# The recurrent steps of a two-block network: bf16 pairs for the diagonals of the tanh recurrence, and gates summed in PSUM in the GRU and the LSTM

## The chip, the cores and the metric

One Trainium2 chip, one of its cores. The metric is the device time of one execution of the whole program, in microseconds (us). It is one program with seven stages in a row, each closed by a barrier of all engines.

## What is computed

The input is `x` (16 sequences of 128 steps of 128 features) and a condition vector per sequence, `cond`, which is the first hidden state of three recurrences. The program computes

```python
x = x + mamba(rnn(x, cond))          # tanh recurrence, then a state-space scan
x = x + ffn(gru(x, cond))
x = x + gla(proj(cond, x))           # gated linear attention
x = x + moe(lstm(x, cond))
```

Three of the stages are recurrences over 128 time steps, where a step needs the hidden state of the step before:

```python
# tanh recurrence
h = tanh(h @ Wh + x_t @ Wx + b)
# GRU
reset, update = split(sigmoid(concat([x_t, h]) @ W + b))
m = x_t @ Wx + bx + reset * (h @ Wh + bh)
h = update * h + (1 - update) * tanh(m)
# LSTM
i, f, o = sigmoid(...); g = tanh(...)       # four gates of x_t @ Wx + b + h @ Wh
c = f * c + i * g
h = o * tanh(c)
```

## The kernel before, in words

Features lie on the 128 partitions and the 16 sequences (`N`) along the free axis, so one hidden state is a 128x16 tile. The order of work is written out by hand for each engine, and semaphores carry every dependence: `e.wait_ge(vec, ...)` holds the engine's queue until VectorE has counted that far. Register work (addresses that depend on the loop's counter, values to wait for) stands in the same queues as `ISA` or `REGISTER_ALU`. A recurrence is a loop whose body holds several steps: 8 in the tanh recurrence, 16 (`STEPS`) in the other two.

**The tanh recurrence** (`rnn`) reproduces the reference's sums in a set order of additions, which makes a step long: about 40 us. To get the exact products of a weight row with h, h is cut into three bf16 pieces (`pieces`, lines 122 to 140), and for each piece a "diagonal" of 128x512 is built (L127): the identity, folded to 32 columns (`id32`, float32), times the piece, broadcast along the columns. VectorE's order in `pieces` is: cast of h to piece 0 (L131), remainder (L134), diagonal 0 (L127), cast 1 (L138), remainder, diagonal 1, cast 2, diagonal 2. TensorE (`h_product`, L263) multiplies them with the weights: 12 matmuls with diagonal 0, 8 with diagonal 1, 4 with diagonal 2, each group after a wait on `diagh`. ScalarE copies the four banks out (L395). VectorE, behind `pieces`, does the prefix sums of a later step's input part (`x_prefix(g)`: a scan at L497 and an add at L501), and then waits for ScalarE's fourth copy before the prefix scan of h's products (`prefix_odd(R)`, also L497). The rest of the step (differences, chains, the tanh written out in some 40 small VectorE operations) follows on VectorE.

**The GRU** (`gru`) first computes the input part of all gates for all steps into `gx` (three blocks of 128x2048). Then, for each step: TensorE multiplies h with the weights of reset and update and with `gwh` (three float32 matmuls of 16 columns, L998; the trace shows each as two), and counts `prod` once, after the third; it then issues 6 (`WARM`) matmuls of 512 columns on an idle tile whose result nobody reads (L1001). VectorE adds the input part to both gates (L1028); ScalarE takes one sigmoid of both (L1013); VectorE computes reset times the third product (L1031), adds the input part (L1034); ScalarE takes the tanh (L1015); VectorE computes h - th (L1036), times update (L1038), plus th (L1040), which is the new h and releases TensorE.

**The LSTM** (`lstm`) has the same form: four matmuls (L1080), one count, 6 idle matmuls (L1083), one addition of the input part for four gates (L1110), a sigmoid of three gates (L1095) and a tanh of one (L1096), f*c (L1113), i*g (L1115), their sum (L1117), a tanh (L1098), and o times it (L1119), the new h.

## Time and profile before

| what | value |
|---|---|
| time, median of 3 runs | 8900.65 us (8898.45 to 8903.1) |
| the profiled execution | 8898.33 us, its span 8896.5 us |
| tanh recurrence, loop | 249 to 5407 us |
| GRU, loop | 7548.0 to 7951.3 us |
| LSTM, loop | 8255.0 to 8631.0 us |
| busy over the span: PE, DVE, ACT | 70%, 85%, 48% |

The engines are PE (TensorE), DVE (VectorE), ACT (ScalarE), POOL (GpSimd) and SP. In a row of the timeline the first number is the start in us from the start of the span, the second the duration in us, then engine, line of the kernel, operation, `out<-in`, shapes and count; in brackets how long the engine had been idle, and what released it. A row with `x4` is four instructions merged: its duration is from the first one's start to the last one's end. Each loop has 128 steps.

### The profile page before, as it was taken

What the parts mean: (1) busy time and instruction counts of PE and PEld (TensorE: products, weight loads), DVE (VectorE), ACT (ScalarE), POOL (GpSimd) and SP (SyncE); (2) the same over time, 40 slices, a digit from 0 to 9 for tenths busy, and PEclk for the clock granted to TensorE, in tenths of its full rate; (3) what the DMA queues carried; (4) which work ended last, traced back from release to release, by engine and by line L of the source; (5) the groups of instructions that cost most, each with busy time, mean ns of one, the idle gap of its engine ahead of it and who ended that gap; (6) DMA issues with size and microseconds to landing.
All of it is one profiled execution on the core that took longest, in us unless ns stands there. A gap on an engine that the chain in (4) does not pass through costs nothing. (4 is left out here: it accounts for less than half of the span.)

```text
span 8896.5 us, 108600 instructions
## 1 busy us (share of the span) xinstructions
PE 6269.1 (70%) x33921; PEld 2486.1 (28%) x34193; DVE 7600.0 (85%) x12570; ACT 4291.4 (48%) x4428; POOL 1329.7 (15%) x1111
## 2 busy tenths in 40 slices
PE   5677777676767676767676764488888887662779
PEld 1222222222222222222222221122222222331443
DVE  5999999999999999999999996899999997336223
ACT  3666666665656665656665663233333332112222
POOL 0000000000000000000000000377777774000000
PEclk8888888888888888888888887799999999995999
DMA  0000000000000000000000000000000000000000
GB/s 6 1 1 1 1 1 1 1 1 1 1 1 1 1 1 1 1 1 1 1 1 1 1 1 22 17 3 4 4 4 4 4 4 3 0 6 3 3 14 5
DMA packets 14002, 27.97 MB, mean 3 GB/s; under 512 B 3665, under 2 KB 11602, under 8 KB 12434
## 3 DMA queue, kind: packets, MB, share of 16 engines
q1 hardware_dynamic: 13586, 22.47, 0.9%
q8 instruction: 256, 4.19, 0.2%
q14 instruction: 160, 1.31, 0.0%
HBM read 15.12 MB, written 7.34 MB: 3 GB/s over the span
## 5 line engine op out<-in xcount | busy, mean ns | idle before, releaser
L901 POOL TENSOR_TENSOR hc<-hh,cg 128x512 f32<-128x512 f32 x1024 | 1296.2, 1268 | 506.9 <-DVE hh L884 506.9
L829 ACT ACTIVATE ps_m<-ps_m,aneg 128x508 f32<-128x508 f32 x1024 | 673.4, 658 | 1188.6 <-DVE hh L884 1063.5
L884 DVE TENSOR_TENSOR_SCAN hh<-ps_m,bx 128x512 f32<-128x512 f32 x1024 | 1232.9, 1209 | 0.0
L800 PE MATMUL ps_m<-hc,pick 128*128 128x512 f32 x2048 | 1051.1, 597 | 2.1 <-POOL hc L901 0.8
L508 DVE TENSOR_TENSOR_SCAN co<-rx_d 128x772 f32<-128x772 f32 x544 | 915.4, 1745 | 0.0
L508 DVE TENSOR_TENSOR_SCAN co<-rh_d 128x3088 f32<-128x3088 f32 x128 | 843.8, 6592 | 31.8 <-ACT rh_d L366 28.6
L263 PE MATMUL r_ps<-rh_diag,whq 32*128 32x512 bf16 x3072 | 360.1, 624 | 666.9 <-DVE rh_diag L127 611.5
L866 DVE TENSOR_TENSOR bx<-ps_m,bg 128x512 f32<-128x512 f32 x1024 | 675.3, 664 | 45.9 <-PE ps_m L813 45.8
L439 POOL TENSOR_TENSOR r_gate<-ident 128x1 f32<-128x1 f32 x16 | 5.7, 356 | 4576.1 <-PE r_ps L255 4576.1
L255 PE MATMUL r_ps<-wdiag,xsp 32*128 32x512 bf16 x3312 | 311.4, 528 | 517.8 <-DVE rh_gain L171 186.4
L274 PE MATMUL r_ps<-rh_diag,whn 32*128 32x512 bf16 x4608 | 438.5, 548 | 267.9 <-ACT rh_pd L395 267.9
L281 PE MATMUL r_ps<-rh_s,negid 128*128 128x512 f32 x1024 | 524.3, 658 | 85.2 <-DVE rh_s L501 85.1
L811 PE MATMUL ps_m<-rows,ones 128*128 128x512 bf16 x944 | 371.0, 393 | 249.1 <-ACT ps_m L829 248.4
L281 PE MATMUL r_ps<-rx_s,negid 128*128 128x512 f32 x1096 | 507.9, 607 | 7.9 <-DVE rx_s L501 7.9
L366 ACT ACTIVATE rx_d<-r_ps 128x1024 f32<-128x1024 f32 x274 | 402.3, 1550 | 212.3 <-PE r_ps L287 212.3
L284 PE MATMUL r_ps<-rx_pd,ident 128*128 128x512 f32 x1096 | 492.7, 592 | 0.0
L395 ACT ACTIVATE rh_pd<-r_ps 128x512 f32<-128x512 f32 x512 | 266.1, 604 | 456.9 <-PE r_ps L263 456.6
L360 ACT ACTIVATE rx_d<-rx_s 128x2048 f32<-128x2048 f32 x137 | 417.7, 3049 | 106.6 <-DVE xwt L526 102.9
L284 PE MATMUL r_ps<-rh_gain,ident 128*128 128x512 f32 x1024 | 460.2, 592 | 0.0
L398 ACT ACTIVATE rh_sg<-r_ps 128x2048 bf16<-128x2048 f32 x128 | 240.3, 1878 | 452.4 <-PE r_ps L274 452.4
L800 PEld LDWEIGHTS ps_m<-hc,pick 128*128 128x128 f32 x2048 | 389.8, 191 | 173.4 <-POOL hc L901 21.6
L497 DVE TENSOR_TENSOR_SCAN rx_s<-rx_pd 128x1040 f32<-128x1040 f32 x137 | 317.7, 2319 | 137.7 <-ACT rx_pd L354 102.2
(389 smaller groups left out, 11206.2 us busy)
## 6 DMA issues: line engine op xcount, KB each, us to landing
rows_scratch<-pc SPq DMA_DIRECT2D x48, 128.0 KB
rows<-rows_scratch SPq DMA_DIRECT2D x128, 48.0 KB
ew<-in_e SPq DMA_DIRECT2D x3, 1024.0 KB, 6.8
co<-in_x_dn SPq DMA_DIRECT2D x1, 1024.0 KB, 4.8
xcur<-in_x_dn SPq DMA_DIRECT2D x1, 1024.0 KB
out_x<-xcur SPq DMA_DIRECT2D x1, 1024.0 KB, 3.9
qi<-in_f_q SPq DMA_DIRECT2D x1, 384.0 KB, 3.1
xpw<-in_xp_t SPq DMA_DIRECT2D x1, 257.0 KB
```

The costliest lines, as they stand in the source:

```text
L274: ins = e.matmul(ps[:, bank0 + b, :], whn[rows(b), q, :], h_mov(b, r), start=False, stop=(i == 8), skip_group_check=True)
L281: e.matmul(ps[:, bank0 + b, :], negid[:], piece(F, "s", b), start=True, stop=False)
L284: e.matmul(ps[:, bank0 + b, :], ident[:], diff(b), start=False, stop=False)
L360: e.activation(F["at"][:, :, :, 2::3], pairs(F["s"][:, :, 2:K2]), ACT.Copy).then_inc(done, 1)
L366: e.activation(remainder_slots(F, first, count, odd), remainder_sums(bank0, first, count, odd), ACT.Copy).then_inc(done, 1)
L508: return e.tensor_tensor_scan(co[:, at], F["d"][:, 0, 1:][:, at], F["d"][:, 1, 0:N * LX][:, at], 0.0, ALU.add, ALU.add)
L800: e.matmul(ps[:, 6, :], pick[:, 128 - un:256 - un], hc[un % NHC][:], start=False, stop=True, skip_group_check=True).then_inc(summed, 1)
L811: e.matmul(ps[:, un % 2, :], ones3[:], rows[0][b][:, j, :], start=True, stop=True).then_inc(dt_bc, 1)
L829: e.activation(da[un % NDA][:, :, 1:T], ps[:, un % 2, :].rearrange("p (n t) -> p n t", n=NG4)[:, :, 1:T], ACT.Exp, scale=aneg[:, 0:1]).the ...
L866: e.tensor_tensor(bx[un % NBUF][:], ps[:, 2 + un % 2, :], bg[:], ALU.mult).then_inc(driven, 1)
L884: e.tensor_tensor_scan(hh[un % NBUF][:], da[un % NDA].rearrange("p n t -> p (n t)"), bx[un % NBUF][:], 0.0, ALU.mult, ALU.add).then_inc(sc ...
L901: e.tensor_tensor(hc[un % NHC][:], hh[un % NBUF][:], cg[:], ALU.mult).then_inc(weighted, 1)
```

## The change

Three parts.

1. In `rnn`, the identity is kept in bf16 and repeated for all 16 sequences (`idn`, 128x16x32, one copy in the setup), and each piece of h is written twice side by side (`part` is 128x3x16x2). A diagonal is then a product of two bf16 operands, read in pairs of neighbours. A cast writes 32 elements where it wrote 16. The order of the instructions stays.
2. In `gru` and `lstm`, VectorE copies the next step's input part into PSUM (`seed`), and the matmuls of the gates add onto it (`start=False`). The banks alternate between even and odd steps. ScalarE reads its sums directly from PSUM. The product with `gwh` in the GRU keeps its own bank.
3. The gates are counted and read one by one. In the GRU TensorE's order is reset, `gwh` product, update, with a count after each; the new state is `update*h + sigmoid(-a)*th`, so that `update*h` (`old`) and `1 - update` (`new`, a second ScalarE sigmoid with scale -1) don't wait for the tanh. In the LSTM the input and forget gates are counted first, then the other two. `WARM` is 5 instead of 6.

The diff, cut to its core (the casts and diagonals, the loops of `gru`, the loops of `lstm`):

```diff
-        id32 = sb("id32", [128, KB])
+        id32 = sb("id32", [128, KB]); idn = sb("idn", [128, N, KB], BF16)
-        R.update(part=sb("rh_part", [128, 3, N], BF16), rest=sb("rh_rest", [128, 2, N]),
+        R.update(part=sb("rh_part", [128, 3, N, 2], BF16), rest=sb("rh_rest", [128, 2, N]),
...
+            halves = lambda x: x.rearrange("p n (a c) -> p n a c", c=2)
             def diagonal(q):
-                return tl.inc(e.tensor_tensor(F["diag"][:, q], id32[:].unsqueeze(1).to_broadcast([128, N, KB]),
-                                              F["part"][:, q, :].unsqueeze(2).to_broadcast([128, N, KB]), ALU.mult))
+                return tl.inc(e.tensor_tensor(halves(F["diag"][:, q]), halves(idn[:]),
+                                              F["part"][:, q].unsqueeze(2).to_broadcast([128, N, KB // 2, 2]), ALU.mult))
+            def cast(q, x):
+                return tl.inc(e.tensor_tensor(F["part"][:, q], x.unsqueeze(2).to_broadcast([128, N, 2]),
+                                              nought[:].unsqueeze(2).to_broadcast([128, N, 2]), ALU.add))
...
-WARM = 6
+WARM = 5
...
 # gru, TensorE
-                        e.wait_ge(vec, t * KV + 1)
+                        at = 3 * (step % 2)
+                        e.wait_ge(vec, t * KV + V0)
-                        for q in range(3):
-                            i = e.matmul(ps[:, q, 0:N], gw[:, 1, q * D:(q + 1) * D] if q < 2 else gwh[:], h, start=True, stop=True)
-                        i.then_inc(prod, 1)
+                        e.matmul(ps[:, at, 0:N], gw[:, 1, 0:D], h, start=False, stop=True, skip_group_check=True).then_inc(prod, 1)
+                        e.matmul(ps[:, at + 2, 0:N], gwh[:], h, start=True, stop=True).then_inc(prod, 1)
+                        e.matmul(ps[:, at + 1, 0:N], gw[:, 1, D:2 * D], h, start=False, stop=True, skip_group_check=True).then_inc(prod, 1)
 # gru, ScalarE
-                        e.wait_ge(vec, t * KV + 2)
-                        e.activation(sg[:], gate[:], ACT.Sigmoid).then_inc(act, 1)
-                        e.wait_ge(vec, t * KV + 4)
+                        e.wait_ge(prod, t * KP + 1)
+                        e.activation(reset[:], ps[:, at, 0:N], ACT.Sigmoid).then_inc(act, 1)
+                        e.wait_ge(prod, t * KP + 3)
+                        e.activation(upd[:], ps[:, at + 1, 0:N], ACT.Sigmoid).then_inc(act, 1)
+                        e.activation(new[:], ps[:, at + 1, 0:N], ACT.Sigmoid, scale=-1.0).then_inc(act, 1)
+                        e.wait_ge(vec, t * KV + V0 + 2)
                         e.activation(th[:], r2[:], ACT.Tanh).then_inc(act, 1)
 # gru, VectorE
+                def seed(t, at):
+                    e.tensor_copy(ps[:, at:at + 2, 0:N], gxt[:, 0:2, bass.ds(t, 1), :].rearrange("p q a n -> p q (a n)")).then_inc(vec, 1)
...
-                        e.wait_ge(prod, t + 1)
-                        e.tensor_tensor(gate[:], ps[:, 0:2, 0:N], gxt[:, bass.ds(t, 1), 0:2, :].rearrange("p a q n -> p (a q) n"),
-                                        ALU.add).then_inc(vec, 1)
+                        e.wait_ge(prod, t * KP + 2)
                         e.wait_ge(act, t * KA + 1)
...
+                        seed(t + 1, 3 - at)
                         e.wait_ge(act, t * KA + 2)
-                        e.tensor_tensor(r3[:], at(gh, t), th[:], ALU.subtract).then_inc(vec, 1)
-                        e.wait_ge(vec, t * KV + 5)
-                        e.tensor_tensor(r4[:], r3[:], sg[:, 1, :], ALU.mult).then_inc(vec, 1)
-                        e.wait_ge(vec, t * KV + 6)
-                        e.tensor_tensor(gh[:, bass.ds(t + 1, 1)].rearrange("p a n -> p (a n)"), r4[:], th[:], ALU.add).then_inc(vec, 1)
+                        e.tensor_tensor(old[:], at_t(gh, t), upd[:], ALU.mult).then_inc(vec, 1)
+                        e.wait_ge(act, t * KA + 4)
+                        e.tensor_tensor(r4[:], new[:], th[:], ALU.mult).then_inc(vec, 1)
+                        e.wait_ge(vec, t * KV + V0 + 5)
+                        e.tensor_tensor(at_t(gh, t + 1), r4[:], old[:], ALU.add).then_inc(vec, 1)
...
 # lstm, TensorE
-                        for q in range(4):
-                            i = e.matmul(ps[:, q, 0:N], lwh[:, q * D:(q + 1) * D], h, start=True, stop=True)
-                        i.then_inc(prod, 1)
+                        for q, bank, lo in ((0, 0, 0), (1, 0, N), (3, 1, N), (2, 1, 0)):
+                            i = e.matmul(ps[:, at + bank, lo:lo + N], lwh[:, q * D:(q + 1) * D], h, start=False, stop=True,
+                                         skip_group_check=True)
+                            if q in (1, 2):
+                                i.then_inc(prod, 1)
 # lstm, ScalarE
-                        e.wait_ge(vec, t * KV + 2)
-                        e.activation(s3[:], gate[:, 0:3, :], ACT.Sigmoid).then_inc(act, 1)
-                        e.activation(gg[:], gate[:, 3, :], ACT.Tanh).then_inc(act, 1)
+                        e.wait_ge(prod, t * KP + 1)
+                        e.activation(keeps[:].rearrange("p a n -> p (a n)"), ps[:, at, 0:2 * N], ACT.Sigmoid).then_inc(act, 1)
+                        e.wait_ge(prod, t * KP + 2)
+                        e.activation(gg[:], ps[:, at + 1, N:2 * N], ACT.Tanh).then_inc(act, 1)
+                        e.activation(out_[:], ps[:, at + 1, 0:N], ACT.Sigmoid).then_inc(act, 1)
...
```

How it moves the instructions. First VectorE in one step of the GRU loop, before (`gate` is the sum of gates and input part, the first `r` r1, the second r2, then r3 and r4):

```order
L1028 REGISTER_ALU [waits g_prod]
L1028 TENSOR_TENSOR gate<-ps_g,gx 128x32
L1030 ISA
L1031 SCALAR_TENSOR_TENSOR r<-ps_g,gb,sg 128x16 [waits g_act]
L1033 ISA
L1034 ISA [waits g_vec]
L1034 TENSOR_TENSOR r<-r,gx 128x16
L1035 REGISTER_ALU
L1036 TENSOR_TENSOR r<-gh,th 128x16 [waits g_act]
L1037 REGISTER_ALU
L1038 TENSOR_TENSOR r<-r,sg 128x16 [waits g_vec]
L1039 REGISTER_ALU
```

and with the change (`COPY ps_g` is the seed of the next step):

```order
L1049 ISA [waits g_prod]
L1050 SCALAR_TENSOR_TENSOR r<-ps_g,gb,reset 128x16 [waits g_act]
L1052 ISA
L1053 ISA [waits g_vec]
L1053 TENSOR_TENSOR r<-r,gx 128x16
L1041 ISA
L1041 COPY ps_g<-gx 128x2x16
L1055 REGISTER_ALU
L1056 TENSOR_TENSOR old<-gh,upd 128x16 [waits g_act]
L1057 REGISTER_ALU
L1058 TENSOR_TENSOR r<-new,th 128x16 [waits g_act]
L1059 REGISTER_ALU
```

The addition of `gate` at the head is gone, and the copy into PSUM stands behind r2 with register work ahead of it; behind it come `old` and the product with the tanh, each after its own wait for ScalarE.

ScalarE in the first step of a turn of the GRU loop, before and, in the second fence, with the change (a table load stands at the head of every turn, 16 steps):

```order
L1013 ACT_TABLE_LOAD
L1013 ACTIVATE sg<-gate 128x32 [waits g_vec]
L1014 REGISTER_ALU
L1015 ACTIVATE th<-r 128x16 [waits g_vec]
L1012 ISA
```

```order
L1024 ACT_TABLE_LOAD
L1024 ACTIVATE reset<-ps_g 128x16 [waits g_prod]
L1025 REGISTER_ALU
L1026 ACTIVATE upd<-ps_g 128x16 [waits g_prod]
L1027 ACTIVATE new<-ps_g 128x16
L1028 ISA
L1029 ACTIVATE th<-r 128x16 [waits g_vec]
```

The one sigmoid of both gates, released by VectorE, has become three of one gate each, released by TensorE; the tanh stands behind all three.

VectorE in one step of the LSTM loop, before and, in the second fence, with the change:

```order
L1110 REGISTER_ALU [waits l_prod]
L1110 TENSOR_TENSOR lgate<-ps_l,lgx 128x64
L1112 ISA
L1113 TENSOR_TENSOR lfc<-ls,lcc 128x16 [waits l_act]
L1114 REGISTER_ALU
L1115 TENSOR_TENSOR lig<-ls,lgg 128x16 [waits l_act]
L1116 ISA
L1117 TENSOR_TENSOR lcc<-lfc,lig 128x16 [waits l_vec]
L1118 REGISTER_ALU
L1119 ISA [waits l_act]
L1119 TENSOR_TENSOR gh<-ltc,ls 128x16
```

```order
L1144 TENSOR_TENSOR lfc<-lkeeps,lcc 128x16 [waits l_act]
L1136 ISA
L1136 COPY ps_l<-lgx 128x2x32
L1146 REGISTER_ALU
L1147 TENSOR_TENSOR lig<-lkeeps,lgg 128x16 [waits l_act]
L1148 ISA
L1149 TENSOR_TENSOR lcc<-lfc,lig 128x16 [waits l_vec]
L1150 REGISTER_ALU
L1151 REGISTER_ALU [waits l_act]
L1151 TENSOR_TENSOR gh<-ltc,lout 128x16
```

The addition at the head is gone, and the copy into PSUM stands between f*c (`lfc`) and i*g (`lig`), again with register work ahead of it.

## Rows read from the trace of the kernel before

**Rows 1.** Windows: us, busy (x count) of PE, PEld, DVE, ACT, POOL, clock, DMA.
```profile
249.00:5407.00 5158.00, 3668.78 (x24975) 1414.72 (x25092) 4977.77 (x8576) 3163.82 (x2448) 25.64 (x64) 0.83 0.00 1
7548.00:7951.30 403.30, 272.15 (x1504) 150.58 (x1536) 144.34 (x769) 67.17 (x264) 0.00 (x0) 1.00 0.00 0
8255.00:8631.00 376.00, 300.55 (x1760) 179.13 (x1792) 109.58 (x641) 82.34 (x392) 0.00 (x0) 1.00 0.00 0
```

**Rows 2.** Groups by line, VectorE: name, shapes, count, busy us, mean ns.
```profile
L127 DVE TENSOR_TENSOR rh_diag<-id,rh_part 128x512 bf16<-128x512 f32 x387 | 265.8, 687 | 4.4
...
L171 DVE TENSOR_TENSOR rh_gain<-rh_gain,xq 128x352 f32<-128x352 f32 x128 | 66.3, 518 | 0.0
...
L178 DVE TENSOR_TENSOR rh_gain<-cf,rh_gain 128x176 f32<-128x176 f32 x128 | 42.7, 334 | 0.0
...
L871 DVE COPY bg<-bm 128x512 f32 x4 | 1.8, 460 | 0.8 <-issue 0.3 <-DVE hh L884 0.2
```

**Rows 3.** Timeline, one tanh step: start us, us, engine, line, operation.
```profile
2704.64 0.17 DVE L131 TENSOR_TENSOR rh_part<-h,nought 128x16 bf16<-128x16 f32 x1
...
2704.95 0.68 DVE L127 TENSOR_TENSOR rh_diag<-id,rh_part 128x512 bf16<-128x512 f32 x1
...
2705.69 2.75 PE L263 MATMUL r_ps<-rh_diag,whq 32*128 32x512 bf16 x24 [5.50 <-DVE rh_diag L127]
...
2707.26 2.32 DVE L497 TENSOR_TENSOR_SCAN rx_s<-rx_pd 128x1040 f32<-128x1040 f32 x1
...
2708.46 2.07 ACT L395 ACTIVATE rh_pd<-r_ps 128x512 f32<-128x512 f32 x4 [3.50 <-PE r_ps L263]
...
2710.75 2.32 DVE L497 TENSOR_TENSOR_SCAN rh_s<-rh_pd 128x1040 f32<-128x1040 f32 x1
```

**Rows 4.** Timeline, the first tanh step.
```profile
248.39 2.75 PE L263 MATMUL r_ps<-rh_diag,whq 32*128 32x512 bf16 x24 [0.56 <-ACT xwT L388]
...
253.26 2.33 DVE L497 TENSOR_TENSOR_SCAN rh_s<-rh_pd 128x1040 f32<-128x1040 f32 x1 [2.34 <-ACT rh_pd L395]
```

**Rows 5.** Timeline, one GRU step.
```profile
7702.84 0.61 PE L998 MATMUL ps_g<-gh,gw 128*128 x4 [1.11 <-DVE gh L1040]
...
7703.31 0.37 PE L998 MATMUL ps_g<-gh,gwh 128*128 x2
...
7703.53 1.46 PE L1001 MATMUL ps_g<-g_idle 128*128 128x512 bf16 x6
...
7704.03 0.23 ACT L1013 ACTIVATE sg<-gate 128x32 f32<-128x32 f32 x1 [2.16 <-DVE gate L1028]
7704.30 0.23 DVE L1031 SCALAR_TENSOR_TENSOR r<-ps_g,gb,sg 128x16 f32<-128x16 f32 x1 [0.30 <-ACT sg L1013]
...
7704.89 0.22 ACT L1015 ACTIVATE th<-r 128x16 f32<-128x16 f32 x1 [0.63 <-DVE r L1034]
...
7705.35 0.17 DVE L1038 TENSOR_TENSOR r<-r,sg 128x16 f32<-128x16 f32 x1
...
7705.99 0.61 PE L998 MATMUL ps_g<-gh,gw 128*128 x4 [1.00 <-DVE gh L1040]
```

**Rows 6.** Timeline, one LSTM step.
```profile
8402.33 1.06 PE L1080 MATMUL ps_l<-gh,lwh 128*128 x8 [0.56 <-DVE gh L1119]
...
8403.78 0.24 ACT L1095 ACTIVATE ls<-lgate 128x48 f32<-128x48 f32 x1 [1.91 <-DVE lgate L1110]
8403.92 0.20 ACT L1096 ACTIVATE lgg<-lgate 128x16 f32<-128x16 f32 x1
...
8404.16 0.18 DVE L1115 TENSOR_TENSOR lig<-ls,lgg 128x16 f32<-128x16 f32 x1
...
8405.25 1.06 PE L1080 MATMUL ps_l<-gh,lwh 128*128 x8 [0.56 <-DVE gh L1119]
```

**Rows 7.** Timeline, ScalarE where a GRU loop turn ends.
```profile
7698.97 1.28 ACT L1013 ACT_TABLE_LOAD   x1 [0.26 <-issue]
```

**Rows 8.** One tile's instructions, the GRU's PSUM: ns min/median/max, starts.
```profile
L989 PE MATMUL ps_g<-xcur,gw x16: 592/592/1220, 7534.5 to 7543.2; 128*128 128x512 f32 x16
```

More of the change, by code:

```diff
@@ L124, in pieces @@
         def pieces(tl, e, F, src, dep=None):
+            halves = lambda x: x.rearrange("p n (a c) -> p n a c", c=2)
             def diagonal(q):
-                return tl.inc(e.tensor_tensor(F["diag"][:, q], id32[:].unsqueeze(1).to_broadcast([128, N, KB]),
-                                              F["part"][:, q, :].unsqueeze(2).to_broadcast([128, N, KB]), ALU.mult))
+                return tl.inc(e.tensor_tensor(halves(F["diag"][:, q]), halves(idn[:]),
[3 more added lines that the diff above has]
+                                              nought[:].unsqueeze(2).to_broadcast([128, N, 2]), ALU.add))
             if dep is not None:
                 tl.wait(dep)
-            i = tl.inc(e.tensor_tensor(F["part"][:, 0, :], src, nought[:], ALU.add))
+            i = cast(0, src)
             for q in (1, 2):
                 tl.wait(i)
-                j = tl.inc(e.tensor_tensor(F["rest"][:, q - 1, :], src if q == 1 else F["rest"][:, 0, :], F["part"][:, q - 1, :],
+                j = tl.inc(e.tensor_tensor(F["rest"][:, q - 1, :], src if q == 1 else F["rest"][:, 0, :], F["part"][:, q - 1, :, 0],
                                            ALU.subtract))
@@ L137, in pieces @@
                 tl.wait(j)
-                i = tl.inc(e.tensor_tensor(F["part"][:, q, :], F["rest"][:, q - 1, :], nought[:], ALU.add))
+                i = cast(q, F["rest"][:, q - 1, :])
             tl.wait(i)
@@ L462, in _ @@
                 i = tl.inc(e.tensor_tensor(id32[:], id32[:], ident[:, KB * b:KB * (b + 1)], ALU.add))
+            tl.wait(i)
+            tl.inc(e.tensor_copy(idn[:], id32[:].unsqueeze(1).to_broadcast([128, N, KB])))
             tl.inc(e.memset(xpc[:, :, T * N:], 0.0))
@@ L966, in gru @@
         gw = sb("gw", [128, 2, 2 * D]); gwx = sb("gwx", [128, D]); gwh = sb("gwh", [128, D]); gb = sb("gb", [128, 4])
-        gx = sb("gx", [128, 3, COLS])
-        gate = sb("gate", [128, 2, N]); sg = sb("sg", [128, 2, N]); r1 = sb("r1", [128, N]); r2 = sb("r2", [128, N])
-        th = sb("th", [128, N]); r3 = sb("r3", [128, N]); r4 = sb("r4", [128, N])
+        gx = sb("gx", [128, 3, COLS + N])
+        reset = sb("reset", [128, N]); upd = sb("upd", [128, N]); new = sb("new", [128, N])
+        r1 = sb("r1", [128, N]); r2 = sb("r2", [128, N]); th = sb("th", [128, N]); old = sb("old", [128, N]); r4 = sb("r4", [128, N])
         idle = sb("g_idle", [128, 512], BF16)
@@ L1049, in lstm @@
         lx = sb("lx", [128, 4 * D]); lwh = sb("lwh", [128, 4 * D]); lb = sb("lb", [128, 4])
-        gx = sb("lgx", [128, 4, COLS])
-        gate = sb("lgate", [128, 4, N]); s3 = sb("ls3", [128, 3, N]); gg = sb("lgg", [128, N]); cc = sb("lcc", [128, N])
+        gx = sb("lgx", [128, 4, COLS + N])
+        keeps = sb("lkeeps", [128, 2, N]); out_ = sb("lout", [128, N]); gg = sb("lgg", [128, N]); cc = sb("lcc", [128, N])
         ig = sb("lig", [128, N]); fc = sb("lfc", [128, N]); tc_ = sb("ltc", [128, N])
@@ L1102, in _, with seed @@
                 e.memset(idle[:], 0.0).then_inc(warm, 1)
+                e.memset(gx[:, :, COLS:], 0.0).then_inc(warm, 1)
                 e.wait_ge(moved, 16)
                 e.memset(cc[:], 0.0).then_inc(vec, 1)
-                gxt = gx[:].rearrange("p q (t n) -> p t q n", n=N)
+                gxt = gx[:].rearrange("p (b q) (t n) -> p t b q n", n=N, q=2)
+                def seed(t, at):
+                    e.tensor_copy(ps[:, at:at + 2, 0:2 * N].rearrange("p b (q n) -> p b q n", n=N),
+                                  gxt[:, bass.ds(t, 1)].rearrange("p a b q n -> p (a b) q n")).then_inc(vec, 1)
+                seed(0, 0)
                 with e.Fori(0, T // STEPS) as block:
@@ L1108, in _ @@
                         t = STEPS * block + step
-                        e.wait_ge(prod, t + 1)
-                        e.tensor_tensor(gate[:], ps[:, 0:4, 0:N], gxt[:, bass.ds(t, 1)].rearrange("p a q n -> p (a q) n"),
-                                        ALU.add).then_inc(vec, 1)
                         e.wait_ge(act, t * KA + 1)
-                        e.tensor_tensor(fc[:], s3[:, 1, :], cc[:], ALU.mult).then_inc(vec, 1)
+                        e.tensor_tensor(fc[:], keeps[:, 1, :], cc[:], ALU.mult).then_inc(vec, 1)
+                        seed(t + 1, 2 - 2 * (step % 2))
                         e.wait_ge(act, t * KA + 2)
-                        e.tensor_tensor(ig[:], s3[:, 0, :], gg[:], ALU.mult).then_inc(vec, 1)
-                        e.wait_ge(vec, t * KV + 4)
+                        e.tensor_tensor(ig[:], keeps[:, 0, :], gg[:], ALU.mult).then_inc(vec, 1)
+                        e.wait_ge(vec, t * KV + V0 + 3)
                         e.tensor_tensor(cc[:], fc[:], ig[:], ALU.add).then_inc(vec, 1)
-                        e.wait_ge(act, t * KA + 3)
-                        e.tensor_tensor(lh[:, bass.ds(t + 1, 1)].rearrange("p a n -> p (a n)"), tc_[:], s3[:, 2, :], ALU.mult).then_inc(vec, 1)
+                        e.wait_ge(act, t * KA + 4)
+                        e.tensor_tensor(lh[:, bass.ds(t + 1, 1)].rearrange("p a n -> p (a n)"), tc_[:], out_[:], ALU.mult).then_inc(vec, 1)
 AXX = mybir.AxisListType.X
```

32 lines of the change are left out of this document (20 added, 12 removed).

## The prediction

> **What bounds the kernel now.** I read the windows of the three recurrent loops first [rows 1], then the groups by line [rows 2] and the timelines of single steps [rows 3 to 6]. The tanh loop takes 5158 us and VectorE is busy for 4978 of them: 40.3 us a step, VectorE's to give. The GRU takes 403.3 us (3.15 a step) with VectorE busy 144, ScalarE 67, and TensorE 272, of which most is idle work; the LSTM takes 376.0 us (2.94 a step), busy 110, 82 and 301. No engine is full there: a step is a chain of short operations, each waiting for the one before. So in the first loop I ask what VectorE saves and what it then waits for; in the other two I add up the chain.
>
> **The diagonals.** A 128x512 diagonal takes 0.69 us [rows 2], 387 in all, three a step. The trace has no product of two 16-bit operands. The nearest rows: a copy of 512 elements at 0.46 us, which shows VectorE taking two elements at a time; and, for an operation that takes as many steps as 256 elements, 0.42 us, interpolated between 176 (0.334) and 352 (0.518) [rows 2]. The upper end is no change, 0.69. I take 0.46. The wider casts add 16 elements each, at (0.518 - 0.334)/176 us that is 0.02.
>
> VectorE alone would save 3 x 0.23 - 0.05 = 0.64 us a step. The path does not. In rows 3 the cast starts at 2704.64, diagonal 0 at +0.31; TensorE starts at 2705.69, 0.06 after its end, and takes 2.75; ScalarE follows after 0.02, and VectorE's scan of h's products starts at 2710.75, +6.11. TensorE's 2.75 are not a wait for diagonals 1 and 2: in the first step all three were long there, and it took 2.75 too, with the scan 4.87 after TensorE's start and held by ScalarE [rows 4]. So only diagonal 0 shortens that path. With the change the scan can start at 0.31 + 0.02 + 0.46 + 0.06 + 4.87 = +5.72. VectorE arrives there at +2.62 (the input's scan, 2707.26) - 0.64 + 3.49 (from that scan to h's, 2710.75) = +5.47, and now waits 0.25 for ScalarE's fourth copy. The gain is 6.11 - 5.72 = 0.39 us a step, **50 us** in 128. Behind the scan nothing changes length; the next waits for TensorE and ScalarE count from it. Ends: at 0.42 a diagonal it is 0.43, 55 us; at 0.69 VectorE's path gives +6.16, 6 us lost.
>
> The Trainium skill, "VectorE: DVE Perf Modes", section "The perf-mode tier table", gives a tensor_tensor of 16-bit operands two elements a cycle; by its formula (256 + 151)/0.96 GHz a diagonal would be an estimated 0.42 us and the term 55 us. No row here shows it.
>
> **The GRU.** In rows 5 TensorE's first pass starts at 7702.84; four passes take 0.61 and each 0.26, so they start 0.12 apart, the fifth at +0.47 (7703.31), and the sixth ends at +0.84. The reset product (two passes) is thus ready at +0.38, the second product at +0.61, the third at +0.84. ScalarE's wait behind TensorE was 0.02 in rows 3; VectorE's here 0.13 (from +0.84 to the sigmoid at +1.19 there are 0.35, of which the addition and its hand-over take 0.22). I give ScalarE 0.05: reset runs +0.43 to +0.65. VectorE needs it and the second product (+0.61 + 0.13), and has register work between the two waits: r1 at +0.76, against +1.46 before (7704.30). From there to the tanh 0.59 as before: +1.35, end +1.57. ScalarE's two other sigmoids start at +0.89 and 0.14 later (two in a row start so far apart in rows 6) and end at +1.25, before r2. h - th falls away: r4 started 0.24 after the tanh's end (7705.11 to 7705.35) and can start after 0.04, +1.61; from r4 to the next matmul 0.64 as before: +2.25 against 3.15.
>
> The seed is the term no row shows: nothing of VectorE writes PSUM here. It stands between r2 (from about +1.14) and `old`, whose cover is the tanh's round trip, up to +1.61. At the cost of an operation of 32 elements, about 0.19 (0.334 less 144 elements), with 0.12 of register work ahead, seed and `old` fill that cover to the brim; I let r4 slip by 0.05. Gain 0.90 - 0.05 = 0.85 a step, **109 us**. Ends: no slip, 115 us; a seed as dear as the 512-element copy (0.46), 0.3 of slip, 77 us.
>
> **The LSTM.** In rows 6 the passes start at 8402.33, the last ends at +1.06; the second gate is ready at +0.61 as above. The first sigmoid is over at +0.66 + 0.24 = +0.90, f*c goes to +1.12, the seed behind it. The tanh of g starts at +1.06 + 0.05, takes 0.20, and i*g follows at +1.35 against +1.83 (8404.16). From there to the next step 1.09 as before; the third sigmoid has 0.4 of room before the last tanh. The seed, twice as large, ends about when i*g could start: 0.03 of slip. Gain 0.45, **58 us**. Ends: 61 us, and 36 us with a seed of 0.46.
>
> **What is added.** The table load at each turn of a loop starts 0.26 after the last tanh and takes 1.28 [rows 7]: it ends 1.54 behind that tanh. The next reset sigmoid will be wanted 0.04 + 0.64 + 0.43 = 1.11 behind it: 0.4 late; in the LSTM about 0.3. Seven turns each: 5 us lost, hidden before by the longer step. The setup copy, two memsets and the first seeds: 1 us. `WARM` 5 saves nothing: the idle matmuls, 0.22 apart (1.46 less 0.38 over 5), end 0.69 + 5 x 0.22 + 0.16 = 1.95 into a step of 2.3, so they delay nobody; 6 would have ended at 2.17.
>
> **Sum.** 50 + 109 + 58 - 6 = 211. The profiled execution took 8898.3 us (span 8896.5, 1.8 around it), so 8687; the median of the runs is 2 us above it: **8689 us**.
>
> **Rivals.**
> 1. *The seed is dear.* Speaking for it: no row of VectorE writing PSUM, and both covers are used up in my own sum. Against: adding the gates from PSUM fitted into 0.22. With 0.46 a seed: GRU 77, LSTM 36, so 54 less: 8743.
> 2. *The diagonals stay at 0.69.* For: the piece is read as one repeated pair, which no row shows at two at a time; nothing in the trace has two 16-bit operands. Against: the repeated element of today costs nothing (0.69 is the rate of one element a cycle). 56 us less: 8745.
> 3. *The pair is fetched anew each time*, so that a diagonal gains half, 0.58: the path gives 6.11 - (0.33 + 0.58 + 4.93) = 0.27 a step, VectorE's own 3 x 0.11 - 0.05 = 0.28: 35 us in place of 50, 8704. The Trainium skill says so much in "Vector Engine (DVE) Microarchitecture Reference", section "5.2 Measured stream behaviour on trn2": full rate only where at least two adjacent 4-byte words come in a run, about 0.65 of a cycle more otherwise; the pair here is one word. The trace speaks against it at one element at a time, and not at two.
> 4. *The other side: the clock falls.* The two gated loops run at a granted clock of 1.00, 2.4 GHz [rows 1], and the idle matmuls are there to hold it. With a fifth of them gone it could sink to 1.2 GHz. A float32 matmul took 592 ns at one level and up to 1220 at the other [rows 8]; so passes go from 0.12 to 0.24 apart and idle matmuls from 0.22 to 0.43. TensorE alone then needs 6 x 0.24 + 5 x 0.43 = 3.6 us a GRU step and 8 x 0.24 + 2.15 = 4.1 an LSTM step, more than 3.15 and 2.94: 58 and 148 us lost in place of 167 gained, 8898 - 50 + 206 + 1 + 2 = 9057. It turns the whole slower once the low level holds in about 6 of 10 steps (211 of the 167 + 206 that lie between the two cases). Against: TensorE's busy share goes up, from 67% (272/403) to (2.13 - 0.22)/2.3 = 83%, and in the LSTM from 80% to 86%, since the steps shrink more than the work.
> 5. *More than forecast*: no slips and 0.42 a diagonal, 55 + 115 + 61 - 6 = 225, or 8675; with ScalarE's wait at 0.02 and cheaper register work, some 0.1 more a gated step, 8650.
>
> **Chances.** Forecast as it stands (8665 to 8710, rival 3's time inside it) 0.62, of which rival 3 has 0.08; rival 1 0.14; rival 2 0.11; rival 5 below 8665 0.09; rival 4 0.03; the rest 0.01. The range runs from 8645 to 8746. About 0.2% of the time (18 us) is what a measurement can tell from no change: faster 0.95, same 0.02, slower 0.03.
>
> **What would show it.** The group of diagonals at about 0.46 us in place of 0.69; a wait of VectorE for ScalarE's copy ahead of h's scan, some 0.25 us in each of 128 steps, where there was none; GRU loop near 300 us and LSTM near 320; the copies into PSUM near 0.2 us; r4 right behind the tanh; the clock at 1.00 in both loops. The forecast is wrong if a seed takes more than 0.3 us, if `old` ends after the tanh, if h's scan starts more than 5.9 us behind the cast, or if the clock drops.

## The result, and the profile after

The changed kernel takes 8888.63 us at the median of 20 runs (8796.22 to 8912.55), the kernel before 8904.15 (8889.69 to 8915.56): a ratio of 0.9955, 95% interval 0.9936 to 0.9974. The ratio goes by the means, 8862 and 8903 us: 0.45% faster where 2.4% were forecast. The medians differ by 16 us alone, 0.17%, and the new one lies 143 us above the end of the range.

The times of the changed kernel fall into groups: eight from 8796 to 8819 us with a mean granted clock over the span of 0.838 to 0.843, eleven from 8885 to 8913 us with 0.823 to 0.827, and one between (8847 us, 0.834). (The granted clock is TensorE's, as a share of full speed: 1.00 is 2.4 GHz, 0.50 is 1.2 GHz, and what lies between is an average over both.) The profiled execution, 8803.29 us (span 8801.5, mean clock 0.842), is one of the first group. So what the trace shows is the faster group.

First the windows of its loops (the columns are those of [rows 1]): tanh, GRU, the LSTM's first 29 us, and the rest of the LSTM. The tanh row begins at the loop's first copy of h, 38 us later in the loop than the one of [rows 1], so the two lengths can't be subtracted.

```profile
287.00:5341.00 5054.00, 3626.70 (x24908) 1407.64 (x24908) 4859.67 (x8535) 3138.87 (x2431) 24.93 (x64) 0.84 0.00 1
7487.00:7773.00 286.00, 246.32 (x1408) 137.99 (x1408) 129.83 (x768) 93.36 (x520) 0.00 (x0) 1.00 0.00 0
8077.00:8106.00 29.00, 26.75 (x138) 17.23 (x139) 9.24 (x54) 8.31 (x43) 0.00 (x0) 0.81 0.00 0
8106.00:8535.00 429.00, 429.00 (x1527) 288.61 (x1527) 104.47 (x589) 88.08 (x478) 0.00 (x0) 0.50 0.00 0
```

Against [rows 1] the GRU loop went from 403.3 to 286.0 us. The LSTM loop went from 376.0 to 458, and the last row says why: the granted clock is 0.50, which is 1.2 GHz, and TensorE is busy for all of the 429 us. The tanh loop became 67 us shorter: from one copy of h into `hs` to the next it is 39.766 us on the mean where it was 40.295, hence 0.53 in each of 127 steps. 67 + 117 - 82 is 102 us, and the two profiled executions are 95 us apart; the other 7 us were lost outside the loops.

**The tanh loop.** VectorE's groups of the changed kernel, as in [rows 2]:

```profile
L505 DVE TENSOR_TENSOR_SCAN rh_s<-rh_pd 128x1040 f32<-128x1040 f32 x127 | 295.1, 2324 | 23.0 <-ACT rh_pd L401 21.7
...
L129 DVE TENSOR_TENSOR rh_diag<-idn,rh_part 128x512 bf16<-128x512 bf16 x384 | 161.5, 421 | 6.0
```

A diagonal takes 0.421 us in place of 0.687. The scan of h's products now has 23.0 us of idle time before it, 21.7 of them for ScalarE's copies. One step, the timeline that answers to [rows 3]:

```profile
2714.60 0.19 DVE L133 TENSOR_TENSOR rh_part<-h,nought 128x32 bf16<-128x32 f32 x1
...
2715.09 0.43 DVE L129 TENSOR_TENSOR rh_diag<-idn,rh_part 128x512 bf16<-128x512 bf16 x1
...
2715.57 2.75 PE L269 MATMUL r_ps<-rh_diag,whq 32*128 32x512 bf16 x24 [5.80 <-DVE rh_diag L129]
...
2718.35 2.06 ACT L401 ACTIVATE rh_pd<-r_ps 128x512 f32<-128x512 f32 x4 [3.44 <-PE r_ps L269]
...
2720.45 2.32 DVE L505 TENSOR_TENSOR_SCAN rh_s<-rh_pd 128x1040 f32<-128x1040 f32 x1 [0.23 <-ACT rh_pd L401]
```

TensorE starts 0.97 after the cast where it was 1.05, and still takes 2.75. The scan starts 5.85 after the cast here; the median of 127 steps is 5.67, against 6.10 before.

**The GRU.** One step of the changed kernel, the answer to [rows 5]:

```profile
7652.56 0.39 PE L1007 MATMUL ps_g<-gh,gw 128*128 x2 [0.29 <-DVE gh L1060]
...
7652.99 0.18 ACT L1024 ACTIVATE reset<-ps_g 128x16 f32<-128x16 f32 x1 [1.07 <-PE ps_g L1007]
...
7653.32 0.23 DVE L1050 SCALAR_TENSOR_TENSOR r<-ps_g,gb,reset 128x16 f32<-128x16 f32 x1 [0.90 <-PE ps_g L1008]
...
7653.86 0.19 DVE L1041 COPY ps_g<-gx 128x32 f32 x1
7653.92 0.22 ACT L1029 ACTIVATE th<-r 128x16 f32<-128x16 f32 x1 [0.22 <-DVE r L1053]
...
7654.17 0.18 DVE L1058 TENSOR_TENSOR r<-new,th 128x16 f32<-128x16 f32 x1
...
7654.78 0.39 PE L1007 MATMUL ps_g<-gh,gw 128*128 x2 [0.29 <-DVE gh L1060]
```

From matmul to matmul 2.22 us, against 3.15. The seed (`COPY ps_g<-gx`) takes 0.19 us and r4 starts 0.03 behind the tanh: the seed delays nothing that shows.

**The LSTM** at both levels of the clock; first a step early in its loop (2.39 us from L1102 to L1102), where before it was 2.92 [rows 6], then one in the 429 us:

```profile
8084.75 1.06 PE L1102 MATMUL ps_l<-gh,lwh 128*128 x8 [0.23 <-DVE gh L1151]
...
8085.66 1.24 PE L1107 MATMUL ps_l<-l_idle 128*128 128x512 bf16 x5
...
8085.77 0.23 DVE L1136 COPY ps_l<-lgx 128x64 f32 x1
8085.85 0.18 ACT L1122 ACTIVATE lgg<-ps_l 128x16 f32<-128x16 f32 x1 [0.25 <-PE ps_l L1102]
...
8086.06 0.18 DVE L1147 TENSOR_TENSOR lig<-lkeeps,lgg 128x16 f32<-128x16 f32 x1
...
8087.14 1.06 PE L1102 MATMUL ps_l<-gh,lwh 128*128 x8 [0.24 <-DVE gh L1151]
...
8253.46 0.17 DVE L1151 TENSOR_TENSOR gh<-ltc,lout 128x16 f32 x1 [0.37 <-ACT ltc L1125]
...
8254.37 1.73 PE L1102 MATMUL ps_l<-gh,lwh 128*128 x8
...
8255.94 2.29 PE L1107 MATMUL ps_l<-l_idle 128*128 128x512 bf16 x5
...
8257.11 0.18 DVE L1151 TENSOR_TENSOR gh<-ltc,lout 128x16 f32 x1 [0.37 <-ACT ltc L1125]
```

At the low level h is ready at 8253.63 (8253.46 and 0.17), and TensorE begins its next product 0.74 later, behind the idle matmuls of the step before; no wait stands in brackets there. The step is 3.65 us (8253.46 to 8257.11), set by TensorE alone: the idle matmuls, which cost nothing at 2.4 GHz, are on the path at 1.2.

### The profile page after: what moved, and what is told of

Its sections match the earlier page's. It is cut to its first block and busy times, and to the rows that moved or that the text cites. A ratio compares the mean times of both kernels' runs of the same rounds, so it can differ in the third digit from the quotient of the medians.

```text
span 8801.5 us, 108877 instructions
## 1 busy us (share of the span) xinstructions
PE 6413.0 (73%) x33937; PEld 2607.2 (30%) x33937; DVE 7505.0 (85%) x12575; ACT 4331.1 (49%) x4812; POOL 1329.5 (15%) x1111
## 5 line engine op out<-in xcount | busy, mean ns | idle before, releaser
L269 PE MATMUL r_ps<-rh_diag,whq 32*128 32x512 bf16 x3072 | 360.1, 624 | 662.3 <-DVE rh_diag L129 628.8
L819 PE MATMUL ps_m<-rows,ones 128*128 128x512 bf16 x1024 | 404.7, 395 | 269.7 <-ACT ps_m L837 265.2
L287 PE MATMUL r_ps<-rh_s,negid 128*128 128x512 f32 x1024 | 507.5, 641 | 57.4 <-DVE rh_s L509 57.0
L287 PE MATMUL r_ps<-rx_s,negid 128*128 128x512 f32 x1096 | 508.3, 607 | 7.9 <-DVE rx_s L509 7.9
```

The costliest lines, as they stand in the source:

```text
L287: e.matmul(ps[:, bank0 + b, :], negid[:], piece(F, "s", b), start=True, stop=False)
L819: e.matmul(ps[:, un % 2, :], ones3[:], rows[0][b][:, j, :], start=True, stop=True).then_inc(dt_bc, 1)
```

## The experiments

Twelve kernels. Ratios are to the kernel before on the same chip, with a 95% interval; loop times and clock are those of the profiled execution. The changed kernel itself was not run again beside them, so where they are set against it, a few us can be the chip's or the hour's: the kernel before has medians of 8904 us beside the changed kernel, and of 8898, 8904 and 8898 beside the others.

| kernel | made from | median us | ratio | GRU, LSTM loop us | clock there |
|---|---|---|---|---|---|
| a_w6 | after | 8646.17 | 0.9717 [0.9704, 0.9730] | 286, 306 | 1.00, 1.00 |
| b_w5 | before | 9080.66 | 1.0200 [1.0186, 1.0214] | 479, 479 | 0.52, 0.51 |
| d_only | before | 8823.35 | 0.9908 [0.9894, 0.9922] | 404, 375 | 1.00, 1.00 |
| a_w0 | after | 8793.22 | 0.9886 [0.9866, 0.9907] | 337, 409 | 0.51, 0.51 |
| a_w7 | after | 8644.64 | 0.9708 [0.9690, 0.9726] | 286, 307 | 1.00, 1.00 |
| a_w75 | after | 8643.60 | 0.9708 [0.9694, 0.9722] | 286, 306 | 1.00, 1.00 |
| a_w5_kick | after | 8805.20 | 0.9898 [0.9878, 0.9917] | 321, 427 | 1.00, 0.73 |
| a_w6_rnn8 | a_w6 | 8711.95 | 0.9782 [0.9768, 0.9797] | 286, 306 | 1.00, 1.00 |
| a_p64 | after | 8683.93 | 0.9752 [0.9735, 0.9768] | 301, 329 | 0.92, 0.91 |
| a_p71 | after | 8905.41 | 1.0004 [0.9995, 1.0014] | 417, 432 | 0.53, 0.64 |
| b_p73 | before | 9050.50 | 1.0164 [1.0147, 1.0181] | 457, 472 | 0.70, 0.66 |
| b_w33 | before | 8904.66 | 1.0006 [0.9996, 1.0015] | 403, 376 | 1.00, 1.00 |

**One idle matmul more, or less (a_w6, b_w5).** My theory after the result: the sixth idle matmul of a step holds the clock, and everything else of the change works. The rival: the new steps bring the clock down by themselves. a_w6:

```diff
-WARM = 5
+WARM = 6
```

> The changed kernel with 6 idle matmuls a step in place of 5. Theory C (the five idle matmuls are one too few to hold TensorE's clock at the new step lengths, whatever the rest does): clock 1.00 in both gated loops in every run, GRU loop 286 us and LSTM loop about 308 us (128 x 2.38 and some table loads), tanh loop as in the changed kernel; 8650 us, all runs within 10 us of each other. Rival S (the new form of the step, short and accumulating onto copied sums, loses the clock whatever the idle matmuls): the same scatter as the changed kernel, 8795 to 8912, median about 8889. Rival F (six idle matmuls no longer fit into the shorter steps): clock held but GRU and LSTM steps some 0.1 us longer, 8675.

Windows of a_w6, the GRU loop and the LSTM loop:

```profile
7477.00:7763.40 286.40, 274.10 (x1536) 150.62 (x1536) 129.88 (x769) 93.47 (x520) 0.00 (x0) 1.00 0.00 0
8068.00:8374.50 306.50, 302.64 (x1792) 179.13 (x1792) 112.91 (x641) 95.78 (x520) 0.00 (x0) 1.00 0.00 0
```

The clock stays at 1.00 throughout, the time is 8646 us, and the LSTM loop is 306 us in place of 458. The same line the other way round in the kernel before, b_w5:

```diff
-WARM = 6
+WARM = 5
```

> The kernel before with 5 idle matmuls a step in place of 6, nothing else. Theory C: the clock falls in the LSTM, in most runs in the GRU too; at 1.2 GHz the GRU step is about 3.5 us (loop 448, 45 more) and the LSTM step 3.6 (loop 467, 91 more): up to 9036 us, and scattered from run to run. Rival S (it is the new form of the step that loses the clock): clock 1.00 in both loops, 8900 us as before, since the idle matmuls stand beside other work.

```profile
7543.00:8022.60 479.60, 449.85 (x1408) 233.87 (x1408) 144.53 (x769) 67.27 (x265) 0.00 (x0) 0.52 0.00 0
8324.00:8804.20 480.20, 478.13 (x1664) 290.99 (x1664) 109.68 (x641) 82.96 (x393) 0.00 (x0) 0.51 0.00 0
```

Both gated loops of the kernel before sink to 0.50 and take 480 us in place of 403 and 376. So `WARM` 5 by itself costs 183 us there (9080.66 less 8898.04, the kernel before on that chip), 45 more than I had expected at most. The clock is lost to the missing matmul; the reordering of the gates by itself does not lose it, as a_w6 shows.

**The diagonals alone (d_only).** Part 1 of the change in the kernel before, with all else untouched:

```diff
-                return tl.inc(e.tensor_tensor(F["diag"][:, q], id32[:].unsqueeze(1).to_broadcast([128, N, KB]),
-                                              F["part"][:, q, :].unsqueeze(2).to_broadcast([128, N, KB]), ALU.mult))
+                return tl.inc(e.tensor_tensor(halves(F["diag"][:, q]), halves(idn[:]),
+                                              F["part"][:, q].unsqueeze(2).to_broadcast([128, N, KB // 2, 2]), ALU.mult))
...
```

> The kernel before with the diagonals from bf16 pairs alone (GRU and LSTM as before, 6 idle matmuls). Both theories: the tanh loop 65 us shorter, 403 and 376 us in the other two loops at clock 1.00: 8835 us with little scatter. If the scatter of the changed kernel came from the tanh loop, it would show here: runs over 8850.

The medians are 75 us apart (the interval of the ratio makes it 69 to 94), and the tanh loop of its profile is 74 us shorter than before: 5043.3 us from the first to the last copy of h, against 5117.5. That is more than the 50 forecast and the 65 expected here. The clock stays at 1.00 in the gated loops, and no run is over 8831 us: the scatter of the changed kernel does not come from the tanh loop. The loop of a_w6 takes 5043.3 us too, that of the changed kernel's profile 5050.3.

**No idle matmuls (a_w0).**

```diff
-WARM = 5
+WARM = 0
```

> The changed kernel with no idle matmuls at all. Theory C: clock 0.50 throughout both gated loops, but TensorE no longer stands in its own way: only the float32 passes are slower (six or eight of them, 0.2 us apart in place of 0.12), GRU step about 2.6 us (333 us), LSTM step about 3.0 (384 us): 8780 us with little scatter, so below the changed kernel's median of 8889. A rival for the 3.65 us of an LSTM step at the low clock: the chain is slow at the low clock, and not held by the idle matmuls; then the LSTM step stays at about 3.6 us, and 8870 or more.

```profile
7474.00:7811.00 337.00, 185.16 (x768) 172.03 (x768) 130.04 (x768) 93.93 (x520) 0.00 (x0) 0.51 0.00 0
8115.00:8524.50 409.50, 239.29 (x1024) 226.16 (x1024) 113.76 (x642) 96.62 (x521) 0.00 (x0) 0.51 0.00 0
```

The clock is low in both loops and yet the time, 8793 us, is 95 us below the median of the changed kernel. At 1.2 GHz a step without idle matmuls takes 2.63 and 3.20 us; five of them bring the LSTM's to 3.65. Here idle matmuls too few to hold the clock are worse than none: 458 against 409 us in the LSTM loop.

**Seven, and seven and five (a_w7, a_w75).** Is six the edge, and must every step have six? a_w7 has `WARM = 7`; a_w75 alternates:

```diff
-WARM = 5
+WARM = 6
...
-                        for _ in range(WARM):
+                        for _ in range(WARM + 1 - 2 * (step % 2)):
```

> The changed kernel with 7 idle matmuls a step. Theory C: the clock stays at 1.00 as with 6; in the GRU the seventh ends (0.69 + 7 x 0.22 = 2.2 us) just as the next step of 2.21 wants TensorE, in the LSTM (0.91 + 7 x 0.22 = 2.45) 0.07 us late: 8646 + 128 x 0.07 = 8655 us. If 6 were already too many (rival F), 7 would cost a whole 0.22 us a step in both loops more: 8700.

> The changed kernel with 7 idle matmuls in even steps and 5 in odd ones, so 6 on average, in steps of 2.21 and 2.38 us. Theory B (what counts is the emptiest stretch: a step with five leaves one that is too empty, whatever the average): clock falls in some runs, and time scatters between 8650 and 8900 as with 5. Theory A (the average of TensorE's columns over several steps decides; here it is that of the kernel with 6, and above that of the kernel before): clock 1.00, 8650 us with little scatter.

Both hold the clock at 1.00 in both loops and take what a_w6 takes. The seventh costs nothing that can be measured. Steps of five do no harm between steps of seven, so it is not the emptiest step that decides.

**A burst every 16 steps (a_w5_kick).** If the clock is only lost by bad luck and a burst brings it back, five a step and a burst now and then would do.

```diff
-                        for _ in range(WARM):
+                        for _ in range(WARM + 24 * (step == 0)):
```

> The changed kernel with 5 idle matmuls, and 24 more in the first step of each turn of 16 steps. Theory H (once down, the clock is held down by the form of the step, though TensorE is busy 100% of it; an unbroken row of wide matmuls brings it back): the clock returns to 1.00 at each turn and falls again some way on, if at all; the extra row costs 24 x 0.22 = 5.2 us a turn at the high clock, so 8646 + 16 x 5.2 = 8729 us if it always holds, and up to 8850 with falls. Rival: the row does not bring it back, each costs 24 x 0.43 = 10.3 us, and both loops stay at 0.50: 8900 + 165 = 9065 us.

```profile
7479.00:7800.10 321.10, 282.49 (x1568) 157.57 (x1600) 129.80 (x769) 93.52 (x520) 0.00 (x0) 1.00 0.00 0
8107.00:8534.00 427.00, 405.71 (x1815) 254.02 (x1856) 113.76 (x642) 96.19 (x520) 0.00 (x0) 0.73 0.00 0
```

The GRU loop holds, 35 us longer through the bursts. The LSTM loop goes down and up, 0.73 on the mean. One burst in it, with the products of a step before and behind:

```profile
8159.90 1.73 PE L1102 MATMUL ps_l<-gh,lwh 128*128 x8
8161.84 8.27 PE L1107 MATMUL ps_l<-l_idle 128*128 128x512 bf16 x28 [0.22 <-issue]
8169.95 0.96 PE L1102 MATMUL ps_l<-gh,lwh 128*128 x8
```

Behind it the eight passes take 0.96 us in place of 1.73: the burst does raise the clock again. But its own time eats the gain. At 8805 us the kernel is no faster than the lower group of the changed kernel. With 24 more in 16 steps it issues 6.5 idle matmuls a step on the mean, more than a_w6, and its LSTM loop loses the clock all the same.

**Long runs or many (a_p64, a_p71, b_p73, b_w33).** Six or seven in a step hold, five do not, and a_w75 leaves two readings: either what counts is how many stand in one run in at least every other step, or how many there are over several steps. The first three change the loop's count, in both gated loops; a_p64:

```diff
-                        for _ in range(WARM):
+                        for _ in range(6 if step % 2 == 0 else 4):
```

a_p71 has 7 and 1 there, b_p73 7 and 3 in the kernel before. b_w33 splits the six of the kernel before:

```diff
-                        for _ in range(WARM):
+                        for _ in range(3):
+                            e.matmul(ps[:, 7, :], idle[:, 0:D], idle[:], start=True, stop=True)
+                        e.wait_ge(vec, t * KV + 4)
+                        for _ in range(3):
                             e.matmul(ps[:, 7, :], idle[:, 0:D], idle[:], start=True, stop=True)
```

> The changed kernel with 6 idle matmuls in the even steps and 4 in the odd ones, so as many in all as with 5 in each. Theory R (what decides in this kernel is how many idle matmuls stand behind one another in at least every other step, and six do it where five do not): both gated loops stay at granted clock 1.00 (GRU 286 us, LSTM 306) and the median is about 8645 us. Theory A (what decides is how many there are over several steps): no better than 5 in each step, so the LSTM loop falls to 0.50 and the times lie at 8796 to 8912 us like those of the changed kernel.

> The changed kernel with 7 idle matmuls in the even steps and 1 in the odd ones: 4 a step on average, fewer than the changed kernel's 5. Theory R (the longest run of idle matmuls decides): clock 1.00 in both gated loops and about 8648 us. Theory A (their number over several steps decides): at least as low a clock as with 5 in each step, loops at 0.50 in part or whole; with fewer idle matmuls a step at 0.50 is shorter than 3.6 us in half of the steps, so about 8800 to 8900 us. As a third outcome the GRU loop may hold and the LSTM loop not, about 8750 us.

> The kernel before with 7 idle matmuls in the even steps and 3 in the odd ones: as many in all as the kernel before with 5 in each step, which ran both gated loops at clock 0.50 and took 9081 us. Theory R (the longest run decides): clock 1.00, about 8903 us, like the kernel before. Theory A (their number over several steps decides): both loops at 0.50, 9050 to 9085 us.

> The kernel before with its 6 idle matmuls a step split into three and three: between them TensorE waits for VectorE's fourth operation of the step (r2 in the GRU, ig in the LSTM), some 0.5 us, and the second three are done before h is ready. Their number is that of the kernel before. Theory R (the longest run decides): the clock falls to 0.50 in both gated loops; the step is then about 3.6 to 3.8 us and the time about 9080 us. Theory A (their number decides): clock 1.00 and about 8903 us.

Windows, GRU and LSTM loop: first b_w33, then b_p73, then a_p71.

```profile
7549.00:7952.70 403.70, 296.25 (x1536) 140.38 (x1536) 144.26 (x769) 67.54 (x265) 0.00 (x0) 1.00 0.00 0
8255.00:8631.40 376.40, 324.71 (x1792) 168.96 (x1792) 109.66 (x641) 82.95 (x393) 0.00 (x0) 1.00 0.00 0
```

```profile
7558.00:8015.10 457.10, 358.12 (x1408) 201.77 (x1408) 144.42 (x769) 67.57 (x265) 0.00 (x0) 0.70 0.00 0
8319.00:8791.20 472.20, 406.77 (x1664) 247.20 (x1664) 109.51 (x641) 82.87 (x393) 0.00 (x0) 0.66 0.00 0
```

```profile
7479.00:7896.50 417.50, 365.30 (x1280) 226.99 (x1280) 130.15 (x770) 94.68 (x521) 0.00 (x0) 0.53 0.00 0
8200.00:8632.00 432.00, 366.66 (x1536) 247.80 (x1536) 113.54 (x641) 96.12 (x520) 0.00 (x0) 0.64 0.00 0
```

Theory R falls three times: six in two runs of three hold the clock at 1.00 and cost nothing that can be measured (8904.66), and runs of seven every other step don't hold it when the steps between have one or three. Theory A has the outcome of these three, though it expected b_p73 at 0.50 throughout, where it is 0.70 and 0.66. Neither had a_p64: R said 1.00 and 8645 us, A said like the changed kernel, and it took 8684 us (8667 to 8714). Its trace, of the slowest of four runs, has 0.92 and 0.91. It also shows a clock that comes back by itself within the GRU loop, where the changed kernel's LSTM loop stayed low to its end:

```profile
7731.00:7769.00 38.00, 38.00 (x132) 23.88 (x131) 12.16 (x72) 7.90 (x48) 0.00 (x0) 0.50 0.00 0
7772.00:7810.00 38.00, 30.80 (x176) 17.27 (x176) 16.38 (x97) 11.53 (x65) 0.00 (x0) 1.00 0.02 3
```

With as many idle matmuls in all, six and four did better than five and five, on another chip. Together with a_w5_kick this says that the mean number per step does not order these kernels either.

**More of them in the tanh loop (a_w6_rnn8).** In that loop the clock averages 0.84, and h's first products run at the low level (24 of them in 2.75 us). Eight idle matmuls ahead of them should bring them forward. The rival, Q: what is won there is lost elsewhere.

```diff
+                    for _ in range(8):
+                        e.matmul(ps[:, 4, :], tau[:, 0, :], xpc[:, 0, 0:512], start=True, stop=True)
                     h_product(0, KD * t)
```

> The changed kernel with 6 idle matmuls, and eight idle bf16 matmuls of 512 columns ahead of the products with the diagonals in each step of the tanh recurrence, into a PSUM bank that is free there; nobody reads them. Theory P (after the change VectorE waits about 0.2 us a step for the chain diagonal 0, TensorE, ScalarE, and TensorE's 2.75 us in it are its low clock of 0.50): at 1.00 the products take about 1.5 us, the wait goes, h's scan starts some 5.4 us behind the cast in place of 5.67, and the time falls by 0.2 to 0.3 us a step, 25 to 40 us: about 8615. Rival Q (the eight do not raise the clock in time and stand in front of the products, or the later products lose by it): no gain, or the products start later and it costs 10 us and more.

It is 66 us slower than a_w6. The products did get faster: at the median they take 1.60 us where they took 2.75, and the scan of h's products starts 5.36 after the cast (median) in place of 5.67. On the mean it starts no earlier, 6.03 against 5.98: in the first step of each turn of eight, the idle matmuls start 1.9 to 4.2 after the cast and 0.43 apart, in front of the products, and the scan comes 9.7 after the cast where it was 8.1. And the groups of TensorE show where the low level went. First a_w6, then a_w6_rnn8, the tanh loop:

```profile
L287 PE MATMUL r_ps<-rh_s,negid 128*128 128x512 f32 x1016 | 494.0, 630 | 58.5 <-DVE rh_s L509 58.2
...
L269 PE MATMUL r_ps<-rh_diag,whq 32*128 32x512 bf16 x3048 | 357.5, 625 | 664.5 <-DVE rh_diag L129 648.4 <-DVE rh_part L133 10.0 <-DVE rh_rest L140 3.4
```

```profile
L287 PE MATMUL r_ps<-rh_s,negid 128*128 128x512 f32 x1016 | 571.6, 715 | 193.5 <-DVE rh_s L511 193.4
...
L269 PE MATMUL r_ps<-rh_diag,whq 32*128 32x512 bf16 x3048 | 223.4, 422 | 43.0 <-DVE rh_diag L129 42.9
```

L269 goes from 625 to 422 ns a matmul, and L287, whose sums ScalarE and VectorE copy next, from 630 to 715. VectorE's waits for the copies and products behind it, from its list of waits, a_w6 and then a_w6_rnn8:

```profile
DVE co L516 <- ACT rh_d L372: 26.2, 37, 1.0
DVE rh_s L505 <- ACT rh_pd L401: 21.7, 96, 0.2
DVE rh_d L558 <- PE r_ps L300: 3.5, 8, 1.1
```

```profile
DVE co L518 <- ACT rh_d L374: 57.1, 63, 1.0
DVE rh_s L507 <- ACT rh_pd L403: 36.3, 32, 2.6
DVE rh_d L560 <- PE r_ps L300: 34.7, 56, 1.0
```

51.4 us before, 128.1 now: 77 us more, of which the loop (5113 against 5043 us between the first and the last copy of h) shows 69. So theory P is wrong and Q is right. The gain had a ceiling anyway: VectorE waited only 22 us for these products. Fewer of them, or another place, weren't tried.

## Why the prediction was wrong

**The diagonals: mechanism right, size small.** Forecast 0.46 us each and 50 us in all; measured 0.421 us and 67 (changed kernel) to 74 (d_only). The wait that I set against VectorE's saving appeared, 0.23 us in the step shown. By 0.42 the forecast's own sum gave 55, and from cast to scan the mean step gained 0.42, 53 us. Some 12 more lie behind the scan (33.80 us on the mean from there to the next cast, 33.89 before). There I had said that nothing changes length, and that is wrong: VectorE's copies of later products wait less for TensorE. Their wait in the tanh loop, first before, then changed:

```profile
DVE rh_d L550 <- PE r_ps L294: 21.7, 15, 1.9
```

```profile
DVE rh_d L558 <- PE r_ps L300: 6.7, 15, 1.1
```

That is 15 us less; the wait of `co` for ScalarE grew by 3 (28.6 to 31.4), and the difference is the 12. In d_only the wait shown is 3.9 us, which fits its 74. Why TensorE is in time for these more often was not tested. Rivals 2 and 3 are out: the repeated pair costs nothing extra. The Trainium skill, "Vector Engine (DVE) Microarchitecture Reference", section "5.2 Measured stream behaviour on trn2", wants at least two adjacent 4-byte words in a run, as measured there on 32-bit numbers; the row of 421 ns shows no such price for a pair of 16-bit numbers read again and again.

**The GRU: right.** Forecast 297 us with its table loads (403 - 109 + 3), measured 286; 0.85 a step forecast, 0.92 measured. The slip of 0.05 for the seed did not come.

**The LSTM: right at the high clock alone.** Forecast 320 us (376 - 58 + 2). With the clock held (a_w6) it is 306; the seed, 0.23 us, ends before i*g could start. Rival 1, the dear seed, is out. With its five idle matmuls the loop took 458 us.

**The table loads: less than forecast.** In the changed kernel:

```profile
7522.36 1.28 ACT L1024 ACT_TABLE_LOAD   x1 [0.19 <-issue]
```

A GRU turn of 16 steps takes 35.77 us where 16 steps of 2.217 (the median) are 35.47: 0.3 late, where I took 0.4. Before it was 50.38 against 16 x 3.142, so 0.1 was there already. In the LSTM loop of a_w6 a turn is 38.27 against 16 x 2.384, 0.1 late, as much as before (46.91 against 16 x 2.922). Of the 5 us that I added, 1 or 2 are there.

**The step that failed is the weight given to rival 4, and in it one argument.** The forecast has both gated loops at 1.00 throughout, so a fall of the clock is in its sum at nothing. I named the mechanism, that with a fifth of the idle matmuls gone the clock could sink to 1.2 GHz, and gave it 0.03, because TensorE's busy share goes up. The share did go up, to 246/286 = 86% in the GRU, which held in this execution. But in the LSTM it was 26.75/29.00 = 92% over the first 29 us, in which the clock fell, where the kernel before held the clock at 80% (300.55/376) and in the GRU at 67%. b_w5 and b_p73 against the kernel before, and a_p71 against a_w6, show it falling with nothing but idle matmuls missing, and a_w6 shows it held. The strongest row against my argument is the last of the first fence: 429 us with TensorE busy without a gap, at 0.50. Busy share as the profile counts it is no guide here. The Trainium skill, "TensorE: Matmul & The Clock Gate", section "Part 1: The HAM clock gate (the "warmup" mystery)", lets the clock go by how busy TensorE has lately been; by the profile's busy time this trace disagrees. "`WARM` 5 saves nothing" was half of a sum: I priced what the edit saves, and left what it could lose to one argument.

The price in rival 4 was too high as well. I had the passes 0.24 apart and the LSTM step at 4.1 us; they are (8255.94 - 8254.37)/8 = 0.20 apart and the step is 3.65. And the outcome is not one case: with the LSTM loop low and the GRU loop high the kernel takes about 8646 + 458 - 306 = 8798 us, which is where the eight lower runs lie. The eleven upper ones have no profile. Their mean clock is 0.015 below the others', over 8900 us as much as some 270 us more at half speed, about the length of a GRU loop: presumably most of that loop is low too. That is worked out and not shown.

**The sum.** In the profiled execution the tanh loop came out 17 us better than forecast, the GRU 11 better, the LSTM 138 worse: 8687 - 17 - 11 + 138 = 8797, and it took 8803; the 6 us are those outside the loops. In a_w6, whose profiled execution took 8644, it is 24, 11 and 14 better, and the same 6 worse. The median would have been 43 us below my forecast, 8646 against 8689.

**What stays open.** Why five a step fail in short steps and six hold in long ones. The kernel before puts 6 idle matmuls into a GRU step of 3.15 us, 1.9 in a microsecond, and keeps the clock; the changed kernel's LSTM puts 5 into 2.39 us, 2.1 in a microsecond, and loses it. No rate of idle matmuls, no mean number per step (a_w5_kick against a_w6, a_p64 against the changed kernel) and no busy share orders all of these runs. What was not varied is what the other matmuls of a step contribute, and what the idle ones multiply: their operands are zeros. Why one program lands in two groups is open too.
